# Where a routing stage takes its reciprocal deviations and scores: GpSimd's power and ScalarE's sigmoid, or logarithms and exponentials on ScalarE

## The reference, cut to what matters

```python
xn = (x - mean(x)) / sqrt(var(x) + 1e-5)            # _layernorm
scores = sigmoid(xn @ gate_w.T)                     # 32 experts
_, topk_ids = top_k(scores + e_bias, 4)
topk_w = scores[topk_ids]; topk_w = topk_w / sum(topk_w)
out = sum over the 4 experts of topk_w * ((silu(xn @ w1) * (xn @ w3)) @ w2)
```

## Time and profile before

| what | value |
|---|---|
| median of 3 runs | 1151.97 us (1151.42 to 1154.69) |
| the profiled execution's own time | 1153.96 us |
| its span, first to last instruction | 1151.9 us |
| busy in the span: PE, DVE, ACT, POOL | 904.1, 732.5, 579.4, 637.3 us |
| mean granted TensorE clock | 0.917 |

### The profile page before, as it was taken

The page is one execution under the profiler, slowest core; times in us unless marked ns, Lnnn a source line. Parts: engine busy times, 40 slices in busy tenths (PEclk is TensorE's granted clock), DMA queues, the critical chain, the costliest instruction groups (busy, mean ns, idle before and its releaser), DMA issues. The chain is left out here.

```text
span 1151.9 us, 28621 instructions
## 1 busy us (share of the span) xinstructions
PE 904.1 (78%) x10913; PEld 713.8 (62%) x10913; DVE 732.5 (64%) x1798; ACT 579.4 (50%) x955; POOL 637.3 (55%) x656
## 2 busy tenths in 40 slices
PE   2478988875666575289996389899899899998998
PEld 1356766653322232089995278888888888886565
DVE  3566777644768584246554566777877778754765
ACT  1156778774766667247664133334434434433554
POOL 1248888772778776534444655546556365412454
PEclk9999899985988787689998589999999999999999
DMA  6222112105756854877765713141332414000010
GB/s 168 78 69 69 58 58 66 48 3 173 281 220 232 281 205 182 320 202 202 201 201 154 273 49 126 70 167 56 141 96 98 170 27 168 14 2 1 20 29 29
DMA packets 103654, 144.12 MB, mean 125 GB/s; under 512 B 13845, under 2 KB 84418, under 8 KB 97122
## 3 DMA queue, kind: packets, MB, share of 16 engines
q1 hardware_dynamic: 69698, 108.72, 27.8%
q0 software_dynamic: 8480, 20.99, 5.3%
q10 hardware_dynamic: 25344, 12.59, 3.6%
HBM read 76.60 MB, written 65.40 MB: 123 GB/s over the span
## 5 line engine op out<-in xcount | busy, mean ns | idle before, releaser
L1467 POOL DMA_INDIRECT rows_x<-rows_r,index_r x128 | 134.3, 1049 | 61.5 <-issue 37.5
L450 POOL TENSOR_TENSOR p_lo_a<-probs_a,p_hi_a 128x1024 f16<-128x1024 f32 x64 | 136.1, 2132 | 47.0 <-ACT p_hi_a L313 47.0
L913 POOL DMA_INDIRECT fetched_a<-rows_y,chosen_row x128 | 125.8, 983 | 63.0 <-DVE att_a L816 31.1
L626 PE MATMUL psum<-v_x_a,probs_a 128*128 128x65 f32 x1024 | 125.0, 276 | 0.0
L626 PEld LDWEIGHTS psum<-v_x_a,probs_a 128*128 128x128 f32 x1024 | 120.9, 194 | 0.0
L1671 POOL TENSOR_TENSOR h_lo_t<-hidden_t,h_hi_t 96x512 f16<-96x512 f32 x48 | 55.6, 1158 | 87.7 <-ACT h_hi_t L1621 87.7
L715 ACT ACTIVATE q_a_a<-psum 128x512 f16<-128x512 f32 x64 | 38.2, 597 | 129.7 <-PE psum L646 129.7
L801 DVE TENSOR_REDUCE negmax_a<-psum 128x8 f32<-128x1024 f32 x64 | 78.3, 1224 | 8.7 <-PE psum L611 3.0
L312 ACT ACTIVATE probs_a<-psum 128x1024 f32<-128x1024 f32 x64 | 65.7, 1026 | 34.8 <-PE psum L170 34.8
L359 DVE TENSOR_REDUCE negmax_a<-psum 128x8 f32<-128x1024 f32 x64 | 77.8, 1215 | 4.7 <-PE psum L186 4.5
L677 PE MATMUL psum<-wo,att_t_a 128*128 128x128 f32 x512 | 64.3, 279 | 17.4 <-DVE q_b_a L785 15.5
(11 more groups left out here) (368 smaller groups left out, 3160.4 us busy)
## 6 DMA issues: line engine op xcount, KB each, us to landing
values<-v_out_r SPq DMA_DIRECT2D x16, 1040.0 KB, 4.2
v_x_a<-values SPq DMA_DIRECT2D x16, 1040.0 KB, 7.6
keys<-k_out_r SPq DMA_DIRECT2D x16, 1024.0 KB, 4.0
listed_t<-rows_x SPq DMA_DIRECT2D x96, 128.0 KB, 2.3
rows_y<-result_t ACTq DMA_DIRECT2D x48, 256.0 KB, 2.2
k_a_a<-keys SPq DMA_DIRECT2D x16, 512.0 KB, 5.5
k_b_a<-keys SPq DMA_DIRECT2D x16, 512.0 KB, 7.6
q_pad_a<-narrow_q SPq DMA_DIRECT2D x64, 64.0 KB
```

Source lines behind the costliest of these rows:

```text
L450: nc.gpsimd.tensor_tensor(p_lo[:, s % RING0, :], probs[:, s % NPR, :], p_hi[:, s % RING0, :], ALU.subtract).then_inc(s_plo, 1)
L626: last_ = nc.tensor.matmul(PV[:, part, i * (HD + 1):(i + 1) * (HD + 1)], probs[:, s % 3, lane(part, i)], v_x[:, par, b % GB, h, :], start= ...
L913: nc.gpsimd.indirect_dma_start(fetched[:, b % NF1, k, :], None, rows_y, bass.IndirectOffsetOnAxis(ap=chosen["row"][:, b, k:k + 1], axis=0) ...
L1467: nc.gpsimd.indirect_dma_start(rows_x, bass.IndirectOffsetOnAxis(ap=index[:, g * GB + t, k:k + 1], axis=0), rows[:, g % 2, t, :, :].rearra ...
```

## The change

The reciprocal deviation leaves POOL. ACT takes `log_var = ln(var + eps)` and `seed = exp(-0.5 * log_var)`, and DVE makes one Newton step of four small operations in `normal`. The sigmoid becomes an exponential on ACT, and an addition of 1 and a reciprocal on DVE at the head of `choose`. ACT calls `reciprocal_deviation(0)` before `masked(0)`, and `reciprocal_deviation(g+1)` at the head of group g, ahead of `keep`'s step 0.

```diff
+                def reciprocal_deviation(g):
+                    act.wait_ge(s_mv, g + 1)
+                    if g >= 2:
+                        act.wait_ge(s_xhat, g - 1)
+                    nc.scalar.activation(log_var[:, g % 2, :], meanvar[:, g % 2, :, 1], ACT.Ln,
+                                         bias=const["eps"][:, :]).then_inc(s_rstd, 1)
+                    act.wait_ge(s_rstd, 2 * g + 1)
+                    nc.scalar.activation(seed[:, g % 2, :], log_var[:, g % 2, :], ACT.Exp, scale=-0.5).then_inc(s_rstd, 1)
+
...
-                    nc.scalar.activation(score[:, g % 2, :, :], LG[g % 2].rearrange("p (t e) -> p t e", e=E0),
-                                         ACT.Sigmoid).then_inc(s_score, 1)
+                    if g:
+                        act.wait_ge(s_score, g)
+                    nc.scalar.activation(expo[:, :, :], LG[g % 2].rearrange("p (t e) -> p t e", e=E0), ACT.Exp,
+                                         scale=-1.0).then_inc(s_expo, 1)
...
                 nc.scalar.activation(ident16[:, :], ident[:, :], ACT.Copy).then_inc(s_set, 1)
+                reciprocal_deviation(0)
                 masked(0)
...
                 for g in range(G):
+                    if g + 1 < G:
+                        reciprocal_deviation(g + 1)
                     keep(g, 0, 11)
...
                     if g:
                         dve.wait_ge(s_lo, g)
+                    y = seed[:, g % 2, :]
+                    after(nc.vector.tensor_tensor(square[:, :], y, y, ALU.mult))
+                    after(nc.vector.scalar_tensor_tensor(square[:, :], meanvar[:, g % 2, :, 1], EPS, square[:, :], ALU.add, ALU.mult))
+                    after(nc.vector.tensor_scalar(square[:, :], square[:, :], -0.5, 1.5, ALU.mult, ALU.add))
+                    after(nc.vector.tensor_tensor(rstd[:, :], square[:, :], y, ALU.mult))
...
                     grade, chose = score[:, g % 2, :, :], mark[:, g % 2, :, :]
+                    dve.wait_ge(s_expo, g + 1)
+                    after(nc.vector.tensor_single_scalar(expo[:, :, :], expo[:, :, :], 1.0, ALU.add))
+                    nc.vector.reciprocal(grade, expo[:, :, :]).then_inc(s_score, 1)
                     dve.wait_ge(s_score, g + 1)
...
-                def reciprocal_deviation(g):
-                    pool.wait_ge(s_mv, g + 1)
-                    if g >= 2:
-                        pool.wait_ge(s_xhat, g - 1)
-                    nc.gpsimd.tensor_tensor(vareps[:, g % 2, :], meanvar[:, g % 2, :, 1],
-                                            const["eps"][:, :].broadcast_to([P, GB]), ALU.add).then_inc(s_rstd, 1)
-                    pool.wait_ge(s_rstd, 2 * g + 1)
-                    nc.gpsimd.tensor_tensor(rstd[:, g % 2, :], vareps[:, g % 2, :],
-                                            const["power"][:, :].broadcast_to([P, GB]), ALU.pow).then_inc(s_rstd, 1)
-
                 nc.gpsimd.memset(ones16[:, :], 1.0)
                 nc.gpsimd.memset(zeros[:, :, :], 0.0).then_inc(s_set, 1)
-                reciprocal_deviation(0)
                 for g in range(G):
-                    if g + 1 < G:
-                        reciprocal_deviation(g + 1)
                     pool.wait_ge(s_index, g + 1)
```

More of the change, by code:

```diff
@@ L1037, in experts0 @@
         stats, meanvar = rt("stats", [P, GB, 6]), rt("meanvar", [P, 2, GB, 2])
-        vareps, rstd = rt("vareps", [P, 2, GB]), rt("rstd", [P, 2, GB])
+        log_var, rstd = rt("log_var", [P, 2, GB]), rt("rstd", [P, GB])
+        seed, square = rt("seed", [P, 2, GB]), rt("square", [P, GB])
+        expo = rt("expo", [P, GB, E0])
         xhat = rt("xhat", [P, GB, D])
@@ L1060, in experts0 @@
         s_split, s_c, s_counted, s_listed = (rsem(n) for n in ("split", "choice", "counted", "listed"))
-        s_pad, s_blank = rsem("pad"), rsem("blank")
+        s_pad, s_blank, s_expo = rsem("pad"), rsem("blank"), rsem("expo")
         XT = [psum[:, n, :].bitcast(F16) for n in range(2)]
@@ L1165, in logits @@
                     if g >= 2:
-                        pe.wait_ge(s_score, g - 1)
+                        pe.wait_ge(s_expo, g - 1)
                     for t in range(GB):
@@ L1326, in normal @@
                         last_ = nc.vector.tensor_scalar(xhat[:, t, :], x_all[:, n * D:(n + 1) * D], meanvar[:, g % 2, t, 0:1],
-                                                        rstd[:, g % 2, t:t + 1], ALU.subtract, ALU.mult)
+                                                        rstd[:, t:t + 1], ALU.subtract, ALU.mult)
                     last_.then_inc(s_xhat, 1)
```

## The result

The changed kernel takes 1179.54 us (median of 4 runs, 1172.74 to 1185.83). The kernel before, run beside it, takes 1152.38 us (median of 4). The ratio is 1.0244, interval [1.0213, 1.0275]: slower by 2.4%. The forecast was 1176.7 with a range of 1167.5 to 1186.

A forecast was written before the change was run, and what follows sets the result against it. The prediction took an ACT-PE-DVE ring, turning once a group, as leading over POOL for most of the block. Terms 2.4 + 16.9 + 1.2 + 0.2 + 4 = 24.7 us on 1151.97 gave 1176.7 us, range 1167.5 to 1186.

The forecast's parts named there:

- the ring of ACT, PE and DVE: Chain from c_hi through index, xhat, upper_rows, transposes and logits to the next c_hi, once a group; period 21.2 us.
- POOL's ring: POOL's turn of 16 scatters a group; without the power it can turn in 21.5 us.
- The loads: Two table loads on ACT in front of c_hi, paid in groups 1 to 6, less idle time: 16.9 us.
- a pair: ACT's logarithm and exponential for one group, each with its table load, in front of c_hi: 3.1 us.
- At the start: From the block's start to group 0's c_hi: new work less the sigmoid's dropped load, 2.4 us later.
- C to U: From start of c_hi to start of upper_rows: 11.66 to about 12.76 us where xhat leads; +1.2 us in sum.
- C(7) to the end: From group 7's c_hi to the block's end: group 7's own choose adds 0.2 us.
- The clock: Behind upper_rows: later xhat lengthens PE's idle time, two of four groups lose full clock; +4 us, bounds 0 and 8.
- U to M: From start of upper_rows to start of the following masked; the predicted +4 us for PE's clock falls here.
- Faster by POOL's queue: Rival: the loads fall into ACT's idle time and POOL's queue counts; about 1149 us, chance 0.04.
- No reload: Rival: loads of a table already there take no time on ACT; 1155 us, chance 0.03.
- A drain at each load: Rival: ACT stands still another 1.28 us around each of 14 loads; about 18 us more, 1195, chance 0.03.

The follow-up runs named there:

- joint_set: Changed kernel with the one table set holding logarithm and exponential loaded, 1 load in the block instead of 16: 1161.36 us, ratio 1.0109.
- loads_later: Changed kernel with ACT's reciprocal_deviation(g+1) one step later, behind c_hi of group g; all 16 loads stay: 1157.48 us, ratio 1.0080.
- loads_doubled: Changed kernel with a second, unused logarithm and exponential behind the first pair, 32 loads in the block: 1199.63 us, ratio 1.0448.
- after_again: The changed kernel once more, unaltered, beside the first experiments: 1178.16 us, ratio 1.0251 to the kernel before.
- after_busy: Changed kernel with eight unused matmuls a group on PE, where it waits for xhat, in groups 0 to 6: 1176.5 us, ratio 1.0211.
- reordered: Changed kernel's arithmetic with one joint table load, the ACT pair behind c_hi, and DVE's new work and statistics moved: 1143.47 us, ratio 0.9960.
- no_newton: Changed kernel without Newton's step, the exponential's value used as it is: 1164.15 us, ratio 1.0137.
- statistics_moved: Kernel before with only statistics(g + 2) moved to between two key steps, in the middle of lower(g, 11, 17): 1149.07 us, ratio 1.0002.
- scores_only: Kernel before with only the scores changed: exponential on ACT, addition and reciprocal on DVE; the power stays on POOL: 1150.80 us, ratio 1.0017.
- before_busy: Kernel before with the same eight unused matmuls a group on PE, as a control: 1152.44 us, ratio 1.0011.
- after_busy_more: Changed kernel with the eight unused matmuls and ten more between the transposes and the wait for turned: 1174.48 us, ratio 1.0180.

## Why the prediction was right

**What bounds the block.** The prediction said that the ring of ACT, PE and DVE sets the turns and that POOL's power is not what decides. POOL's wait for `index` grew from 24.0 to 63.1 us while the block grew by 24.4. That could not be if POOL's ring led.

**The loads.** The term was 16.9 us and measured 16.87. It rests on 3.1 us for a pair (3.02 to 3.06 measured) and on the 0.81 and 0.90 us of idle time that hid a part of it. `joint_set` and `loads_later` removed the term, each in its own way; `loads_doubled` paid it once more. At the start 2.4 was said, 2.04 came and 2.96 in `after_again`. In the first profile the late weights covered the first pair: ACT waited 0.56 us for the first `xhat` there, and then found the weights in memory. In `after_again` it waited 0.16 us for `xhat` and another 1.03 for the weights.

**C to U.** The forecast was +1.2 us in sum and 12.76 us a turn. It came as +1.62, with 12.73 to 12.79 in the six turns 0 to 5. The gains at the end, where the waits for landed scatters and for a conversion vanish, came as well (15.98 to 12.77 in group 4, 13.59 to 11.87 in group 6, where 11.4 was said). Reciprocal and addition were said to take 0.95 and 0.23 us and took 0.953 and 0.231; Newton's step was said to take 0.85 and took 0.76.

**C(7) to the end** went down 0.73 us instead of up 0.2. Up to the first scatter it was +0.19 (7.53 to 7.72), as the prediction said of `choose`. From the first to the last scatter it was 21.80 us in both. The rest, 6.99 to 6.07 us, lies behind the last scatter's issue. No run tests it, and in `after_again` the whole was 36.42 us, 0.1 more than before.

**The clock.** The size, +4 us, was nearly right (+4.64); the reason given was not. The step that failed is "later `xhat` lengthens this idle time by 1.1 us", read as what brings the clock down in two of the four groups 0, 2, 3 and 5. In fact groups 0, 3 and 5 lost it and group 4 lost more of it (+2.26, +2.19, +2.27 and +1.06 us), while groups 1 and 6, slow before, got it back (-2.30 and -0.83). `after_busy` took 1.3 us out of each of these idle times and every stretch kept its length. Nor did the idle time grow by 1.1 us in each group: it changed by +2.04, -0.55, +0.25, +2.14 and +1.97 us in groups 0, 1, 2, 3 and 5, and it grew most where more of the time ahead of it ran at the full clock than before. So the 4 us were the right sum by a wrong mechanism, and that they came out so near was luck. What the runs show is only which kernels have the lower clock (U to M in sum, us):

| kernel | C to U | U to M |
|---|---|---|
| reordered | 85.81 | 49.95 |
| no_newton | 83.13 | 53.95 |
| statistics_moved | 86.60 | 54.02 |
| before | 86.84 | 56.47 |
| scores_only | 87.99 | 58.39 |
| before_busy | 88.54 | 52.89 |
| loads_later | 92.67 | 58.37 |
| after_busy_more | 88.44 | 57.66 |
| loads_doubled | 88.33 | 60.70 |
| after | 88.46 | 61.11 |
| after_again, after_busy | 88.59, 88.59 | 62.10, 62.08 |
| joint_set | 91.75 | 63.51 |

Mostly, the less time from C to U, the less time U to M takes; `before_busy` and `loads_later` don't fit that, and each row is one profile, while the same kernel gave 61.11 and 62.10. Which activity of PE the chip goes by stays open. I can't say from these runs whether PE's work itself, or what DMA and the other engines do at the time, withdraws the clock.

**The rivals.** "Faster by POOL's queue" fell with POOL's 63.1 us of waiting. "No reload" fell with 16 loads at 1283 ns. "A drain at each load" fell with rows that follow within 0.02 us and with `loads_doubled`, where a pair cost its own length.

**Outside the block** the attention ahead of it took 3.06 us longer in the same code, at a granted clock of 0.77 in its last part (200 to 272 us) against 0.86 before (200 to 269), and the rest took 1.5 us less. The prediction had both at nothing. They are not the change's: `after_again` starts the block at 268.01 us, 1.2 us earlier than before the change. Over all the runs, with the same code ahead of it, the block starts at 263.68 to 273.04 us, so parts inside the block are compared here and not whole spans.

## What to carry to other kernels

Before a function moves to ScalarE, count the table loads that the compiled order holds and look at what stands behind them in the queue. Here the two in front of `c_hi` cost 3.1 us a group, one step later nearly nothing, and one line that asks for the table with both functions removes them. An engine with the most work of a block (POOL's 134 us of scatters) is not its bound while it waits for something: taking work from it gained nothing here, and the new work went to the two engines on which it waited. New work on a ring is free only where an engine already waits there. With one load of the joint set and the new work moved into such places, the kernel with the same arithmetic took 1143 us instead of 1178, 0.4% less than the kernel before.

## What the hardware showed that I had not expected

- Filling 1.3 us of PE's idle time in each of seven turns with matmuls changed nothing behind it in the changed kernel: 62.08 against 62.10 us, with the same pattern in every turn.
- The same kernel shows different patterns of the clock from run to run. In two profiles of the changed kernel the stretch of group 0 took 9.70 and 7.44 us, and that of group 2 took 7.44 and 9.74, while C to U and M to C agreed within 0.15 us in every turn.
- The cost of a reciprocal on DVE grows with its columns: 178 ns for 4, 352 for 32 and 953 for 128.
